# Graph attention on one Trainium2 core: one burst for the value product, leads and slot order by row, a ring of five rows

## What is computed

```python
h = max(layernorm(x), 0)                        # x: 8 x 1024 x 256
q, k, v = h @ Wq + bq, h @ Wk + bk, h @ Wv + bv # 8 heads of 32
scores = q @ k.T / sqrt(32) + (1 - adj) * -1e9  # per batch entry and head, 1024 x 1024
out = softmax(scores) @ v
x = x + (out @ Wo + bo)
```

## Time and profile before

| | |
|---|---|
| Median of 3 runs | 1185.55 us (1184.95 to 1186.07) |
| The profiled execution's own time | 1186.05 us |
| Its span (first to last instruction) | 1184.2 us |
| PE matmul busy | 1139.8 us, 96% |
| PE weight loads busy | 879.6 us, 74% |
| ACT busy | 1024.1 us, 86% |
| DVE busy | 953.2 us, 80% |
| POOL busy | 131.7 us, 11% |
| Chain that ended last | PE 83%, ACT 9%, DVE 2% |

### The profile page before, as it was taken

How to read it: one execution, slowest core, us unless ns; L and a number is a source line. 1 busy time by engine, 2 the same in 40 slices (tenths; PEclk the granted TensorE clock), 3 DMA queues, 4 the chain that set the end, 5 groups by cost and what they waited for, 6 DMA issues and landing times.

```text
span 1184.2 us, 28159 instructions
## 1 busy us (share of the span) xinstructions
PE 1139.8 (96%) x10756; PEld 879.6 (74%) x10756; DVE 953.2 (80%) x1731; ACT 1024.1 (86%) x1899; POOL 131.7 (11%) x234
## 2 busy tenths in 40 slices
PE   5599999999999999999999999999999999999997
PEld 4477777777777777777777777777777777777665
DVE  4688888887888878887888878878888888887884
ACT  2589898998989989898988989889898999989995
POOL 4103000030001200030001300003000030001001
PEclk9799999999999999999999999999999999999999
DMA  8432342314223142331513325132241413223101
GB/s 274 139 82 63 73 125 59 97 48 125 69 81 94 48 128 63 80 96 42 139 41 101 80 55 136 45 100 61 73 126 52 102 46 90 73 81 93 25 19 37
DMA packets 76596, 99.51 MB, mean 84 GB/s; under 512 B 17968, under 2 KB 43696, under 8 KB 76464
## 3 DMA queue, kind: packets, MB, share of 16 engines
q1 hardware_dynamic: 75504, 95.10, 30.3%
q0 software_dynamic: 576, 1.57, 0.5%
q10 hardware_dynamic: 384, 1.05, 0.3%
HBM read 22.15 MB, written 8.39 MB: 26 GB/s over the span
## 4 chain that ended last, share of the span: by engine, by line
PE 83%; ACT 9%; DVE 2%; issue 1%; SPq 1%; DMA 0%; ACTq 0%; DVEq 0%
PE ps_turn L657 26%; PE ps_heads L720 20%; PE ps_scores L643 19%; PE ps_side L664 8%; PE ps_side L691 5%; PE ps_side L673 4%; ACT rows L427 4%; ACT turned_a L433 3%; SPq L272 1%; DVE turned_b L511 1%; DVE rows L504 1%; ACT k_hi L443 1%; ACT ht L449 1%; PE ps_heads L706 1%; ACT q_hi L443 0%
## 5 line engine op out<-in xcount | busy, mean ns | idle before, releaser
L504 DVE CUSTOM_DVE_ANT_0 rows<-ps_scores,mask 128x1024 f32<-128x1024 f32 x512 | 621.6, 1215 | 63.1 <-PE ps_scores L643 41.0
L427 ACT ACTIVATE rows<-rows,row_min 128x1024 f32<-128x1024 f32 x512 | 591.0, 1154 | 18.4 <-DVE row_min L504 18.4
L657 PE MATMUL ps_turn<-ident_r,rows_raw 128*128 128x128 f32 x4096 | 478.5, 259 | 14.6 <-ACT turned_a L433 9.0
L657 PEld LDWEIGHTS ps_turn<-ident_r,rows_raw 128*128 128x128 f32 x4096 | 399.5, 141 | 98.3 <-issue 51.1
L433 ACT ACTIVATE turned_a<-ps_turn 128x512 f32<-128x512 f32 x512 | 306.1, 598 | 85.3 <-PE ps_turn L657 85.1
L643 PE MATMUL ps_scores<-k_stack,q_stack 128*128 128x512 f32 x1024 | 359.5, 432 | 12.8 <-DMA k_stack<-start_k_lo 12.2
L511 DVE COPY turned_b<-ps_turn 128x512 f32<-128x512 f32 x312 | 214.6, 688 | 80.0 <-PE ps_turn L657 79.9
L643 PEld LDWEIGHTS ps_scores<-k_stack,q_stack 128*128 128x128 f32 x1024 | 153.7, 189 | 14.8 <-issue 14.6
L403 POOL COPY inv_wide<-row_inv 128x256 f32<-128x256 f32 x64 | 25.7, 401 | 1007.6 <-DVE row_inv L539 981.7
L720 PE MATMUL ps_heads<-turned_a,v 128*32 128x256 f32 x2048 | 123.8, 382 | 1.0 <-ACT inv_wide L453 1.0
L720 PE MATMUL ps_heads<-turned_b,v 128*32 128x256 f32 x2048 | 123.8, 382 | 0.0
(11 more groups left out here) (59 smaller groups left out, 555.1 us busy)
## 6 DMA issues: line engine op xcount, KB each, us to landing
q_stack<-q_hi SPq DMA_DIRECT2D x240, 64.0 KB, 2.0
q_stack<-q_lo SPq DMA_DIRECT2D x240, 64.0 KB, 2.0
k_stack<-k_hi SPq DMA_DIRECT2D x240, 64.0 KB, 2.0
k_stack<-k_lo SPq DMA_DIRECT2D x240, 64.0 KB, 2.0
res<-in_x SPq DMA_DIRECT2D x32, 256.0 KB, 2.7
out<-res SPq DMA_DIRECT2D x32, 256.0 KB, 2.4
xn<-in_x SPq DMA_DIRECT2D x7, 1024.0 KB, 6.3
mask<-in_adj SPq DMA_DIRECT2D x1, 3584.0 KB, 14.6
```

What stands on the lines that cost most here:

```text
L427: nc.scalar.activation(rows[:, m % RING, :], rows[:, m % RING, :], ACT.Exp, bias=row_min[:, m % RING:m % RING + 1], scale=-1.0, accum_out= ...
L504: nc.vector.tensor_tensor_reduce(out=rows[:, m % RING, :], in0=ps_scores[m % 2][:], in1=mask[:, qt, :], scale=1.0, scalar=START_MIN, op0=A ...
L657: tr = nc.tensor.transpose(ps_turn[half][:, k, :].bitcast(F32R), rows_raw[:, i % RING, kt * P:(kt + 1) * P], ident_r[:])
```

## The change

The transposed copy of half b gets as many places as half a (9 instead of 12), the ring of rows five instead of four. PE does both halves of `heads` in slot r = 0 and nothing of it in r = 3. `turn_inv` stands ahead of the side work in r = 7. The leads of scores, mask and exponential are no longer 4, 3 and 1, but are read from a table by r; a slot in which the lead grows works on two rows, one in which it falls works on none (`reach`). Written out, rows worked on per slot, r = 0 to 7: scores 1, 1, 2, 0, 2, 0, 1, 1; masks 2, 1, 0, 2, 1, 0, 1, 1; exponentials 2, 2, 1, 1, 0, 1, 0, 1. On DVE and ACT the place of exponential, high part, copy and finishing step within the slot also depends on r. `norm_heads` moves from r = 4 to the head of r = 1. `STEPS`, `HT_ROWS`, `STATS`, `ACT_COPIES` (13 + 13 instead of 12 + 13 rows) and the slots of POOL's bias adds are new.

```diff
-RING = 4
-SCORES_AHEAD, MASK_AHEAD, EXP_AHEAD = 4, 3, 1
+RING = 5
+SCORES_AHEAD = (5, 5, 6, 5, 6, 5, 5, 5)
+MASK_AHEAD = (5, 5, 4, 5, 5, 4, 4, 4)
+EXP_AHEAD = (2, 3, 3, 3, 2, 2, 1, 1)
+EXP_AT = (0, 0, 0, 0, 2, 1, 1, 0)
+HIGH_AT = (2, 2, 0, 0, 1, 2, 2, 2)
+COPY_AT = (1, 0, 1, 1, 0, 0, 1, 1)
+TAKE_AT = (2, 1, 2, 0, 0, 1, 1, 0)
-PV_ROW = (0, 3)
-INV_ROW, NORM_ROW = 7, 4
-PLACES = (1 + UNIT_ROWS, PARTS + UNIT_ROWS)
+INV_ROW, NORM_ROW = 7, 1
+PLACES = 1 + UNIT_ROWS
 STEPS = (
-    (("o", 2, (1, 2, 3, 3)), ("qk", 0, (4, 4, 5, 5)), ("o", 3, (7, 7, 7, 8)), ("qk", 1, (9, 10, 12, 12)),
-     ("qk", 2, (14, 14, 15, 15)), ("qk", 3, (16, 17, 18, 18)), ("v", 0, (20, 21, 21, 21)),
-     ("v", 1, (22, 22, 25, 26))),
-    (("qk", 0, (0, 1, 1, 2)), ("v", 0, (4, 4, 5, 5)), ("qk", 1, (6, 6, 6, 7)), ("qk", 2, (8, 9, 9, 10)),
-     ("o", 0, (13, 13, 13, 14)), ("qk", 3, (16, 17, 17, 18)), ("v", 1, (20, 21, 23, 26)),
-     ("o", 1, (28, 28, 29, 30))),
+    (("qk", 0, (1, 2, 3, 3)), ("qk", 1, (5, 5, 6, 7)), ("qk", 2, (9, 9, 11, 11)), ("qk", 3, (13, 13, 14, 15)),
+     ("o", 2, (17, 17, 19, 19)), ("v", 0, (21, 21, 22, 23)), ("v", 1, (25, 25, 25, 27)), ("o", 3, (29, 29, 30, 31))),
+    (("qk", 0, (1, 1, 3, 3)), ("qk", 1, (5, 5, 6, 7)), ("qk", 2, (9, 9, 11, 11)), ("qk", 3, (13, 13, 14, 15)),
+     ("o", 0, (17, 17, 19, 19)), ("v", 0, (21, 21, 22, 23)), ("o", 1, (25, 25, 27, 27)), ("v", 1, (29, 29, 30, 31))),
 )
-HT_ROWS = {(0, 29): 0, (0, 30): 1, (1, 5): 2, (1, 6): 3}
+HT_ROWS = {(0, 27): 0, (0, 29): 1, (1, 3): 2, (1, 4): 3}
-STATS = {i: t for t, i in enumerate((3, 7, 8, 10, 20, 22, 23, 24))}
+STATS = (0, 2, 8, 16, 16, 23, 23, 23)
 ACT_COPIES = (
-    (6, 8, 10, 11, 13, 16, 19, 20, 23, 24, 26, 27),
-    (0, 1, 4, 9, 11, 13, 15, 18, 22, 26, 27, 28, 31),
+    (1, 3, 4, 6, 11, 12, 14, 19, 20, 23, 24, 27, 28),
+    (1, 3, 4, 7, 11, 12, 14, 19, 20, 23, 27, 28, 31),
 )
...
+        def reach(ahead, n):
+            return range(n + ahead[(n - 1) % UNIT_ROWS], min(n + ahead[n % UNIT_ROWS] + 1, BATCH * BATCH_ROWS))
...
@@ ACT, slot: EXP_AT 0, 1, 2 = ahead of copy_a, behind copy_a, behind copy_b @@
+                if EXP_AT[r] == 0:
+                    for m in reach(EXP_AHEAD, n):
+                        exp(m)
...
                 copy_a(b, g, i)
+                if EXP_AT[r] == 1:
+                    for m in reach(EXP_AHEAD, n):
+                        exp(m)
                 if i in ACT_COPIES[g]:
                     copy_b(b, g, i)
...
@@ DVE, slot @@
+                if r == NORM_ROW and not (first and u == 0):
+                    norm_heads(unit(b, g, u) - 1, *((g, u - 1) if u else (1 - g, UNITS - 1)))
                 if r == INV_ROW:
                     invert(b, g, u, first)
...
+                for m in reach(MASK_AHEAD, n):
+                    mask_row(m)
...
@@ PE, slot @@
                 turn(b, g, i, 0)
                 turn(b, g, i, 1)
+                for m in reach(SCORES_AHEAD, row(b, g, i)):
+                    scores(m)
-                if r in PV_ROW and not (first and i < UNIT_ROWS):
-                    heads(unit(b, g, u) - 1, u + 1, g if u else 1 - g, PV_ROW.index(r))
+                if r == 0 and not (first and i < UNIT_ROWS):
+                    for half in range(2):
+                        heads(unit(b, g, u) - 1, u + 1, g if u else 1 - g, half)
+                if r == INV_ROW:
+                    turn_inv(b, g, u, first, last)
...
-                if r == INV_ROW:
-                    turn_inv(b, g, u, first, last)
```

More of the change, by code:

```diff
@@ L444, in high_part, with next_high_part @@
                                      ).then_inc(hi_done, 1)
+            def next_high_part(b, g, s):
+                n, (nb, ng) = "qk"[s % 2], next_phase(b, g)
+                for h in range(PARTS):
+                    if s < 2:
+                        act.wait_ge(stacked[n][g][h], stack_count(n, g, h, b + 1))
+                    else:
+                        act.wait_ge(stacked[n][ng][h], stack_count(n, ng, h, nb, 1))
+                high_part(nb, ng, s, hi[s % 2][:])
             def copy_ht(b, s, bank=ps_heads[:]):
@@ L576, in _ @@
                                     ).then_inc(mask_ready, 1)
-            for m in range(MASK_AHEAD):
-                mask_row(m, m, 0)
+            for n in range(MASK_AHEAD[-1]):
+                mask_row(n)
             def slot(b, g, i, first, last):
-                u, r = i // UNIT_ROWS, i % UNIT_ROWS
+                n, u, r = row(b, g, i), i // UNIT_ROWS, i % UNIT_ROWS
+                ended = step_ended(b, g, i)
+                if r == NORM_ROW and not (first and u == 0):
+                    norm_heads(unit(b, g, u) - 1, *((g, u - 1) if u else (1 - g, UNITS - 1)))
                 if r == INV_ROW:
                     invert(b, g, u, first)
-                m = ahead(g, i, MASK_AHEAD)
-                if not (last and m >= BATCH_ROWS):
-                    mask_row(m, row(b, 0, m), m % ROWS // PARTS)
-                kind, s, pieces = side_work(g, i - 1, first, last)
-                if PIECES - 1 in pieces:
-                    nb, ng = next_phase(b, g)
-                    if kind == "qk":
-                        low_part(nb, ng, s, lo[s % 2][:], hi[s % 2][:])
-                    elif kind == "v":
-                        copy_v(nb, ng, s)
-                    elif kind == "o":
-                        finish(out_count(b, g, s), s)
-                if i not in ACT_COPIES[g]:
-                    copy_b(b, g, i)
-                if r == NORM_ROW and not (first and u == 0):
-                    norm_heads(unit(b, g, u) - 1, *((g, u - 1) if u else (1 - g, UNITS - 1)))
-                if g == 0 and i in STATS and not last:
-                    moments(b + 1, STATS[i])
+                if COPY_AT[r] == 0 and i not in ACT_COPIES[g]:
+                    copy_b(b, g, i)
+                if TAKE_AT[r] == 0:
+                    take(*ended)
+                for m in reach(MASK_AHEAD, n):
+                    mask_row(m)
+                if TAKE_AT[r] == 1:
+                    take(*ended)
+                if COPY_AT[r] == 1 and i not in ACT_COPIES[g]:
+                    copy_b(b, g, i)
+                if TAKE_AT[r] == 2:
+                    take(*ended)
+                for t in range(TILES):
+                    if g == 0 and STATS[t] == i and not last:
+                        moments(b + 1, t)
             def tail():
@@ L718, in heads @@
                     for h in range(PARTS):
[L719 removed]
+                        p0, p1 = place(parity, h), place(parity, PARTS + h)
                         mm = nc.tensor.matmul(ps_heads[h * HEAD_DIM:(h + 1) * HEAD_DIM, 0:UNIT_Q]
@@ L753, in _ @@
             pe.wait_ge(bo_ready, 1)
-            for m in range(SCORES_AHEAD):
-                scores(m, m, m >= 2, 1)
+            for n in range(SCORES_AHEAD[-1]):
+                scores(n)
             def slot(b, g, i, first, last):
@@ L760, in slot @@
                 turn(b, g, i, 1)
-                m = ahead(g, i, SCORES_AHEAD)
-                if not (last and m >= BATCH_ROWS):
-                    fills = b + (1 if m < BATCH_ROWS else 2) if m % ROWS < PARTS else None
-                    scores(m, row(b, 0, m), True, fills)
-                if r in PV_ROW and not (first and i < UNIT_ROWS):
-                    heads(unit(b, g, u) - 1, u + 1, g if u else 1 - g, PV_ROW.index(r))
+                for m in reach(SCORES_AHEAD, row(b, g, i)):
[5 more added lines that the diff above has]
+                    turn_inv(b, g, u, first, last)
                 if (g, i) in HT_ROWS and not last:
```

101 lines of the change are left out of this document (53 added, 48 removed).

## The result

| | before | after |
|---|---|---|
| Median | 1185.25 us (4 runs) | 1145.43 us (4 runs, 1145.42 to 1147.03) |
| Span of the profiled execution | 1184.2 us | 1143.6 us |
| PE matmul busy | 96% | 97% |
| ACT busy | 86% | 90% |
| Chain that ended last: PE, ACT, DVE | 83%, 9%, 2% | 92%, 2%, 1% |

The ratio is 0.9667 (95% interval 0.965 to 0.9683): 39.8 us faster, nearly three times the 13.9 us forecast, and outside the range.

The account below looks back on a forecast made before the run. PE was taken to bound the kernel. Six full entries gave -10.8 us, entry 0 -2.2 and entry 7 -0.9: span 1184.2 - 13.9 = 1170.3, median 1171.5 us (1167 to 1178); 8-in-10 range 1163 to 1189.

Parts of the forecast that it names:

- the sum of PE's own work after the change: PE in a full batch entry: group prices add up to 140.0 us after the change, 139.1 before.
- What bounds: Full batch entries: PE bounds, with 139.1 of 142.2 us its own work and about 3.1 us of waits.
- The price of turns behind scores: PE, turns directly behind scores: 0.79 us each instead of 0.64, for 14 turns per entry instead of 6.
- The doubled scores: PE, slots with two rows of scores: 1.06 us for two rows, 0.533 each; 34.1 us per entry before and after.
- The merged burst: PE, both halves of `heads` in one go: 1.5 us less per batch entry, entering a burst costing nothing.
- The waits: PE's waits for other engines in a full entry: 0.4 us after the change, bounds 0 and 3.1.
- A: Rival: PE's waits only move, 3.1 us on 140.0 per entry; 1183 to 1190, say 1185.5 us; chance 0.13.
- B: Rival: ACT comes late around the burst and PE waits each unit, 0.55 us; 1201 us; chance 0.14.
- C: Rival: no waits in full entries (-3), last and first phases gain from greater lead (-4); 1164 us; chance 0.15.
- D: Rival: merged burst does nothing, 0.17 to 0.20 belonging to each 32 instructions; 1183 us; chance 0.03.
- The ends: Kernel's start and lighter phases: +1.0 us at start, -2.3 and -0.9 in entry 0, last phase 0.

Follow-up runs that it names:

- e2: The changed kernel with scores five rows ahead in every slot, so no slot has two rows of scores and none has none: 1172.95 us.
- e3: As e2, but from the second batch entry on ACT copies only two of four blocks of half a: 1160.25 us.
- e4: The changed kernel with exponentials one row ahead in every slot and first in the slot: 1224.03 us.
- e5: The kernel before with one edit, both halves of the value product in slot r = 0: 1255.77 us.
- e12: The changed kernel with only ACT's order within a slot as before (exponentials, high part, copies): 1164.86 us.
- e1: The changed kernel with the row of scores in slot r = 0 between the two halves of the value product: 1169.54 us.

## Why the prediction was wrong

The step that failed is the sum of PE's own work after the change: 140.0 us per batch entry, where the runs show about 135.8. Three of its terms were priced too high, the turn directly behind scores most of all.

**What bounds (right).** PE sets the pace in the steady part; PE's share of the chain rose from 83 to 92%.

**The price of turns behind scores (wrong, -2.1 us per entry).** I priced groups by their neighbours and put 0.79 on 14 turns. They took 0.64, and without this term PE's work would not have grown in my sum. The trace of the kernel before could have told it: in a full entry only three of its six turns directly behind scores take 0.79, one takes 0.69 and two take 1.20. A price that belongs to the neighbour would not vary so. In the 0.79s and the 1.20s alike the weight load starts 0.11 us behind ACT's copy; before a 1.20 ACT has a high part to do first:

```profile
482.13 0.69 ACT L443 ACTIVATE q_hi<-ps_side,bq_col 128x512 fp32r<-128x512 f32 x1
482.71 0.59 ACT L433 ACTIVATE turned_a<-ps_turn 128x512 f32<-128x512 f32 x1
483.42 0.82 PEld L657 LDWEIGHTS ps_turn<-ident_r,rows_raw 128*128 128x128 f32 x8 [0.67 <-issue]
```

I took one row of PE in the chain as proof that PE was working. e2 and e3 show the round trip. That also means that of the old kernel's 139.1 us some 0.9 were waits: PE's need was 138.2, and its waits 4.0 per entry, not 3.1. (The six turns took 5.5 us, where I had 4.7.)

**The doubled scores (mis-sized, -1.1).** I charged two rows at twice one row, 1.07; they take 1.00. The difference is the 0.07 that I had found for side work behind a transpose; it seems to be contained once in every group of scores behind a turn. I had counted it where it was added and not where it was removed.

**The merged burst (mis-sized, -1.0).** I took entering a burst as free from the tail's row of 3.69. That row is counted from the start of its first matmul, whose record alone is 0.38 us, after idle time; the others are counted from the end of the group before. The changed kernel has both: 3.69 in its tail and 3.59 everywhere else. Merged, a burst is 3.59; with 0.13 for entering and 0.17 for leaving the merge is worth 2.4 us per entry, near the 2.7 that I had worked out for a drain on both sides and set aside, not the 1.5 that I took.

Together 140.0 - 2.1 - 1.1 - 1.0 = 135.8, and the measured 136.4 leaves 0.6, where I had taken 0.4 for waits; 0.3 of it are the three turns of 0.73 to 0.74.

**The waits (right in kind and place).** The unit laid out by hand nearly held: ACT at the turns just in time and some 0.1 us late at three of 64, no wait for a transfer in `high_part` of slot 16. By the new prices the 5.8 us per entry are 138.2 - 135.8 = 2.4 of PE's own work and 4.0 - 0.6 = 3.4 of waits. I forecast -0.9 and +2.7.

**Smaller slips.** Not all full entries of the kernel before take 142.2 us: two of the six take 142.6 and 142.8, which makes 0.8 us in all. And 1170.3 + 1.85 - 0.5 is 1171.65, not 1171.5.

**Rivals.** A (the waits move) and B (ACT's order around the burst makes each unit wait) did not come. B was not far off: e4 and e5 show what the burst does where the lead is short, and e12 what ACT's order can cost (+19.5 us), though there in r = 4 and 5 and not around the burst. C named the right direction, but from the waits; its floor was the wrong 140.0, so the range ended at 1163. D falls by e1.

**The ends (right within their bounds).** +1.9 for +1.0 at the start, +1.4 for 0 in the last phase, and -2.3 for -2.3 between.

**What the parts are worth.** Undone one at a time in the changed kernel, they cost 24 (e1, only the price of two bursts and their waits), 28 (leads of scores), 79 (lead of exponentials), 103 (ring and its leads) and 114 us (slot order), against a whole of 40. Done alone in the old kernel, the burst costs 70 and the spread 19. The parts cannot be summed; they are one schedule. A prediction had to lay the whole unit out, and that step was sound.

## What to carry to other kernels

A price that depends on what stands beside an instruction may be a wait in disguise: before using it, look whether some other engine's instruction always ends at the same short distance ahead of the dearer case, whether the price varies with the same neighbour, and whether the dearer case goes with little work since the last turn. Where a PSUM bank goes from PE to another engine and back, the round trip sets a least length for every slot, and moving work from full slots into those that are shorter removes waits without removing any work (e2: 27.5 us for the rows of scores alone). A long burst on the bound engine pays if the others have that much work ready (e4, e5); the leads, the ring and the order within a slot that provide it belong to the same edit.

## What the runs showed of the hardware that was not expected

Between matmuls on the full array and those on 32 columns of it lies a price on both sides: 0.13 us on entering (1.86 against 1.73 for the same 32 instructions) and 0.14 to 0.17 on leaving. A group of ordinary matmuls directly behind transposes costs 0.07 us once: a projection takes 0.93 against 0.86, and two rows of scores take 1.00 where one takes 0.53. Where a turn waits for ACT's copy out of its bank, 0.11 to 0.12 us pass from the end of the copy to PE's weight load, in the kernel before, the changed one, e2 and e3.
